# Cross-attention queries split batch by batch, first tile's by GpSimd, contexts loaded ahead of weights, norms of the last tile in pieces

## What is computed

```python
x = x + _L0_xattn_ref(_layernorm(x, axis=-1), ctx_768, Wq, Wk, Wv, Wo, bo)
x = x + _L0_attn_ref(_layernorm(x, axis=-1), Wq, Wk, Wv, Wo, rel_bias_emb)
x = x + _L0_ffn_ref(_layernorm(x, axis=-1), clip_x, clip_down, w_gate, w_up, w_down)
...
# in _L0_xattn_ref, per head:
scores = jnp.einsum("bhsd,bhkd->bhsk", q, k) * scale
probs = jax.nn.softmax(scores, axis=-1)
out = jnp.einsum("bhsk,bhkd->bhsd", probs, v)
...
# in _L0_ffn_ref:
xq = _act_fake_quant(x, clip_x[0])
gate = jnp.einsum("bsh,ih->bsi", xq, _weight_fake_quant(w_gate))
up = jnp.einsum("bsh,ih->bsi", xq, _weight_fake_quant(w_up))
h = _act_fake_quant(jax.nn.silu(gate) * up, clip_down[0])
return jnp.einsum("bsi,hi->bsh", h, _weight_fake_quant(w_down))
```

## Time and profile before

| | |
|---|---|
| median of 3 runs | 1633.85 us (1632.8 to 1635.03) |
| the profiled execution | 1636.37 us, span 1634.5 us |
| mean granted clock of TensorE | 0.987 |
| busy share of the span | TensorE 96%, its weight loads 79%, VectorE 68%, ScalarE 45%, GpSimd 22% |
| chain that ended last | TensorE 68%, VectorE 12%, issue 12%, ScalarE 4%, DMA 3% |

### The profile page before, as it was taken

How to read it: one execution, slowest core, us unless ns; L and a number is a source line. 1 busy time by engine, 2 the same in 40 slices (tenths; PEclk the granted TensorE clock), 3 DMA queues, 4 the chain that set the end, 5 groups by cost and what they waited for, 6 DMA issues and landing times.

```text
span 1634.5 us, 33087 instructions
## 1 busy us (share of the span) xinstructions
PE 1566.0 (96%) x12242; PEld 1299.2 (79%) x12242; DVE 1114.9 (68%) x2348; ACT 734.6 (45%) x1555; POOL 355.8 (22%) x217
## 2 busy tenths in 40 slices
PE   7999869999999999999999998899999999997989
PEld 6888758888988889888998887777878778775444
DVE  7776656676667766677666776657657665566788
ACT  5554554555545554455545553333122222222755
POOL 0000234443444335343443433000000000000000
PEclk9999999999999999999999999999999999998999
DMA  6898853332333223342333312250310311324022
GB/s 245 321 357 340 322 192 121 134 114 73 137 132 134 85 91 133 133 148 62 114 133 133 137 57 103 78 194 21 103 67 27 118 39 39 115 90 171 1 103 104
DMA packets 80030, 213.37 MB, mean 131 GB/s; under 512 B 5776, under 2 KB 31824, under 8 KB 77136
## 3 DMA queue, kind: packets, MB, share of 16 engines
q1 hardware_dynamic: 79952, 212.27, 36.0%
HBM read 141.86 MB, written 70.39 MB: 130 GB/s over the span
## 4 chain that ended last, share of the span: by engine, by line
PE 68%; DVE 12%; issue 12%; ACT 4%; DMA 3%; SPq 0%; DVEq 0%; POOL 0%; ACTq 0%; POOLq 0%
PE psum_o L663 13%; PE psum_s L640 6%; PE psum_q L640 6%; PE psum_o L678 5%; PE psum_o L1331 5%; PE psum_q L1331 5%; PE psum_o L532 5%; PE psum_q L1371 4%; PE psum_t L1399 4%; PE psum_t L651 2%; DVE qk L1001 2%; PE psum_t L611 2%; PE psum_s L1385 2%; ACT qk L782 1%; PE psum_t L564 1%
## 5 line engine op out<-in xcount | busy, mean ns | idle before, releaser
L663 PE MATMUL psum_o<-pT,c_nat 128*128 128x512 f32 x1152 | 314.1, 410 | 15.4 <-issue 12.2
L663 PEld LDWEIGHTS psum_o<-pT,c_nat 128*128 128x128 f32 x1152 | 207.6, 193 | 51.8 <-DVE pT L900 14.8
L1183 POOL TENSOR_TENSOR c_nat<-c_raw,zero 128x768 fp32r<-128x768 f32 x64 | 95.4, 1490 | 638.0 <-PE psum_o L663 465.4
L1067 DVE TENSOR_SCALAR oT<-psum_o,c_last 128x512 f32<-128x512 f32 x192 | 143.4, 747 | 72.7 <-PE psum_o L663 72.7
L640 PE MATMUL psum_s<-cT,qk 128*128 128x258 f32 x1152 | 170.3, 290 | 5.8 <-DVE qk L1001 1.9
L640 PEld LDWEIGHTS psum_s<-cT,qk 128*128 128x128 f32 x1152 | 153.0, 191 | 15.5 <-DVE cT L900 6.1
L841 ACT ACTIVATE probs<-psum_s,nmax 128x257 f32<-128x257 f32 x128 | 61.1, 478 | 210.9 <-DVE nmax L1082 210.9
L640 PE MATMUL psum_q<-cT,qk 128*128 128x258 f32 x1152 | 154.9, 286 | 0.0
L640 PEld LDWEIGHTS psum_q<-cT,qk 128*128 128x128 f32 x1152 | 144.0, 190 | 5.1 <-issue 5.1
L900 DVE TENSOR_TENSOR pT<-psum_t,pT 128x512 fp32r<-128x512 f32 x128 | 87.7, 686 | 73.5 <-ACT pT L740 73.5
L740 ACT ACTIVATE cT<-psum_t 128x256 fp32r<-128x256 f32 x192 | 67.6, 389 | 126.6 <-PE psum_t L611 126.4
(11 more groups left out here) (263 smaller groups left out, 3101.7 us busy)
## 6 DMA issues: line engine op xcount, KB each, us to landing
qk_by_tile<-staged SPq DMA_DIRECT2D x32, 1536.0 KB, 9.9
raw<-qk_by_tile SPq DMA_DIRECT2D x16, 3072.0 KB, 12.7
c_raw<-in_ctx_dram SPq DMA_DIRECT2D x64, 384.0 KB, 3.3
last_row<-in_ctx_dram SPq DMA_DIRECT2D x64, 192.0 KB, 4.2
out_dram<-x_out SPq DMA_DIRECT2D x32, 256.0 KB, 2.0
x_res<-in_x_dram SPq DMA_DIRECT2D x16, 256.0 KB, 2.6
x_in<-out_dram SPq DMA_DIRECT2D x4, 1024.0 KB, 8.0
x_res<-out_dram SPq DMA_DIRECT2D x16, 256.0 KB, 2.8
```

The lines of the kernel that those rows point to most:

```text
L663: i = pe.matmul(ps[:], c_nat[(b - 1) % 2][:, part, k, m * P:(m + 1) * P], pT[:, moving, k, :], start=(k, part, moving) == (0, 0, 0), stop= ...
L1067: nc.vector.tensor_scalar(oT[:, m, :, (b - 1) % 4, :], ps[:].rearrange("p (s q) -> p s q", q=SQ), c_last[:, (b - 1) % 2, m:m + 1], None, A ...
```

## The change

- Queries are split per batch and score group, in 16 instructions of 128x384 per tile and part instead of four of 128x1536. In batches 1 to 3 of a tile the parts for the next tile's batches 0 to 2 are made (in batch 3 ScalarE also makes those of batch 3, whose low parts follow in the next tile's batch 0). TensorE waits for each score group's part.
- In the first tile GpSimd makes both parts of batches 0 to 2, and the low part of the output weights. Group 3 of the projection has all its `Q` chunks first and then all its `QK` chunks.
- GpSimd subtracts the next context's last key before it splits the present one, not after.
- SyncE loads contexts and tile 1's queries ahead of the weights.
- In the last tile the statistics and the norm are spread in pieces over batches 1 to 3, and w2q's low part comes at the tile's end.
- The reloads for the feed-forward part are spread over three output tiles, and 54 transposes whose result nobody reads stand in three places of TensorE's queue.

```diff
+        if s == 3:
+            u += [(("Q", s, j), ("o0", "o1")[j % 2]) for j in range(4, 8)]
+            u += [(("CT", "start", c), ("t0", "t1")[c % 2]) for c in range(3)]
         for gp in range(2):
-            if gp:
+            if gp and s < 3:
                 u += [(("Q", s, j), ("o0", "o1")[j % 2]) for j in range(4, 8)]
...
-            if b == 0:
-                pe.wait_ge(s_qlo, 4 * t + (rg + 1))
+            pe.wait_ge(s_qlo, 16 * t + 4 * b + (rg + 1))
             ps, done = empty(pe, U1(("S", b, rg), t, section))
...
+        def raw_of(b, rg):
+            return raw[:, :, rg, :].rearrange("p h (c b q) -> p b c h q", c=KC, q=SQ)[:, b, :, :, :]
+        def qk_of(part, b, rg):
+            return qk[:, part, rg, :, b, :].rearrange("p c (h q) -> p c h q", h=4)
+        def act_qk_high(act, t, b):
             act.wait_ge(s_qraw, 16 * t + 16)
-            nc.scalar.activation(qk[:, 0, rg, :, :, :].rearrange("p c b (h q) -> p h (c b) q", h=4),
-                                 raw[:, :, rg, :].rearrange("p h (a q) -> p h a q", q=SQ), ACT.Copy).then_inc(s_qhi, 1)
+            for rg in range(4):
+                nc.scalar.activation(qk_of(0, b, rg), raw_of(b, rg), ACT.Copy).then_inc(s_qhi, 1)
...
+            act.wait_ge(s_qhi, 12)
+            act_qk_high(act, 0, 3)
...
                 if after:
                     ctxT(b, 2)
-                if section == "first" and b in (1, 2):
-                    act_wo_high(act, b - 1)
+                if b and more:
+                    act_qk_high(act, t + 1, b - 1)
+                if b == 3 and more:
+                    act_qk_high(act, t + 1, 3)
+                if section == "first" and b >= 2:
+                    act_wo_high(act, b - 2)
...
+        def dve_qk_low(dve, t, b, groups):
+            for rg in groups:
+                dve.wait_ge(s_qhi, 16 * t + 4 * b + (rg + 1))
+                nc.vector.tensor_tensor(qk_of(1, b, rg), raw_of(b, rg), qk_of(0, b, rg).bitcast(F32),
+                                        ALU.subtract).then_inc(s_qlo, 1)
...
-                qk_next = b == 3 and more
+                qk_next = b > 0 and more
                 row_max(b, 0)
+                if b == 0:
+                    dve_qk_low(dve, t, 3, range(2))
                 if section == "first" and b == 0:
                     nc.vector.memset(cT[1][:, :, :, 2 * P:SKP].bitcast(F32), 0.0).then_inc(s_zero, 1)
                 if before:
                 row_max(b, 1)
                 if before:
                     dve_probsT(dve, t, b, 1, section)
+                if b == 0:
+                    dve_qk_low(dve, t, 3, range(2, 4))
                 inverse(b, 0)
                 if b == 1 and begun:
                     dve_wv(dve, t, 0, section)
                 inverse(b, 1)
                 if b == 1 and begun:
                     dve_wv(dve, t, 1, section)
+                if not more and b == 2:
+                    dve_group_stats(dve, GROUPS, x_in2, range(2, GROUP))
+                if not more and b == 3:
+                    rsqrt_turn(own_ln, group_ln, group)
                 row_max(b, 3)
                 inverse(b, 2)
-                if qk_next:
-                    dve_qk_low(dve, t + 1, 0, section)
                 if before:
                     dve_attended(dve, t, b, 0, section)
                 inverse(b, 3)
-                if qk_next:
-                    dve_qk_low(dve, t + 1, 1, section)
+                if not more and b == 3:
+                    dve_group_norm(dve, GROUPS, x_in2, x_in2, range(2))
                 if after:
                     ctxT(b, 0)
                     ctxT(b, 1)
                 norm(b, 2)
                 norm(b, 3)
+                if not more and b == 2:
+                    rsqrt_start(own_ln, group_stats, group_ln, group)
                 if before:
                     dve_attended(dve, t, b, 1, section)
                 if qk_next:
-                    dve_qk_low(dve, t + 1, 2, section)
-                    dve_qk_low(dve, t + 1, 3, section)
+                    dve_qk_low(dve, t + 1, b - 1, range(2))
                 if not more and b == 3:
-                    dve_weight(dve, "q")
+                    dve_group_norm(dve, GROUPS, x_in2, x_in2, range(2, GROUP))
                 if b == 3 and begun:
                     dve_x_out(dve, t, section)
                 if after:
                     ctxT(b, 2)
                 if before:
                     dve_attended(dve, t, b, 2, section)
-                if section == "first" and b >= 2:
-                    dve_wo_low(dve, b - 2)
+                if qk_next:
+                    dve_qk_low(dve, t + 1, b - 1, range(2, 4))
                 if not more and b == 1:
-                    dve_group_stats(dve, GROUPS, x_in2)
-                    dve_group_rsqrt(dve, GROUPS)
+                    dve_group_stats(dve, GROUPS, x_in2, range(2))
                 if not more and b == 2:
-                    dve_group_norm(dve, GROUPS, x_in2, x_in2)
+                    for _ in range(2):
+                        rsqrt_turn(own_ln, group_ln, group)
+            if not more:
+                dve_weight(dve, "q")
...
+        def pool_first_queries(pool, b):
+            G = nc.gpsimd
+            nothing = zero[:].rearrange("p (a b c) -> p a b c", a=1, b=1).to_broadcast([P, KC, 4, SQ])
+            for rg in range(4):
+                G.tensor_tensor(qk_of(0, b, rg), raw_of(b, rg), nothing, ALU.add).then_inc(s_qhi, 1)
+            for rg in range(4):
+                pool.wait_ge(s_qhi, 4 * b + (rg + 1))
+                G.tensor_tensor(qk_of(1, b, rg), raw_of(b, rg), qk_of(0, b, rg).bitcast(F32), ALU.subtract).then_inc(s_qlo, 1)
+        def pool_wo_low(pool, h):
+            pool.wait_ge(s_wohi, h + 1)
+            part = slice(4 * h, 4 * h + 4)
+            nc.gpsimd.tensor_tensor(wo_low[:, part, :], wo_raw[:, part, :], wo_high[:, part, :].bitcast(F32),
+                                    ALU.subtract).then_inc(s_wolo, 1)
+        def pool_first_tile(pool):
+            pool_less_last(pool, 0, 0)
+            pool_less_last(pool, 0, 1)
+            full(pool, project(("Q", GROUPS - 1, 7)))
+            pool.wait_ge(s_qraw, 16)
+            for b in range(3):
+                pool_first_queries(pool, b)
+            pool_split(pool, 0, 0, "first")
+            full(pool, U1(("S", 0, 0), 0, "first"))
+            pool_split(pool, 0, 1, "first")
+            for b in range(2, 4):
+                pool_less_last(pool, 0, b)
+                pool_split(pool, 0, b, "first")
+            pool_less_last(pool, 0, 4)
+            for h in range(2):
+                pool_wo_low(pool, h)
         def pool_cross_tile(pool, t, section):
-            if section == "first":
-                pool_less_last(pool, t, 0)
             for b in range(4):
-                pool_split(pool, t, b, section)
                 if section != "last" or b < 3:
                     pool_less_last(pool, t, b + 1)
-                if b == 1 and section != "first":
+                pool_split(pool, t, b, section)
+                if b == 1:
                     pool_bias(pool, t)
...
+        def sp_first_tile(sp):
             sp.wait_ge(s_nat, 1)
             load_ctx(sp, 0, 2)
+            sp.wait_ge(s_qlo, 16)
+            load_qk(sp, 0, 1)
+            sp.wait_ge(s_nat, 2)
+            full(sp, U1(("CT", 0, 2), 0, "first"))
+            load_ctx(sp, 0, 3)
             for i in range(4):
                 sp.wait_ge(s_staged[i], 32 * GROUPS)
-            sp.dma_start(wv[:], Wv.rearrange("(k p) n -> p k n", p=P)).then_inc(s_wvo, 16)
-            sp.dma_start(wo_raw[:], Wo.rearrange("(k p) n -> p k n", p=P)).then_inc(s_wvo, 16)
-            sp.dma_start(bo_all[:], bo.rearrange("(a n) -> a n", a=1).to_broadcast([P, D])).then_inc(s_wvo, 16)
+            sp.dma_start(wo_raw[:], Wo.rearrange("(k p) n -> p k n", p=P)).then_inc(s_wo, 16)
+            sp.dma_start(bo_all[:], bo.rearrange("(a n) -> a n", a=1).to_broadcast([P, D])).then_inc(s_wo, 16)
             sp.dma_start(x_res[:], rows(x_rows, 0)).then_inc(s_xres, 16)
+            sp.wait_ge(s_nat, 3)
+            load_ctx(sp, 0, 4)
+            sp.dma_start(wv[:], Wv.rearrange("(k p) n -> p k n", p=P)).then_inc(s_wv, 16)
+            sp.wait_ge(s_nat, 4)
+            load_ctx(sp, 0, 5)
...
-                        sp.dma_start(wdT[:].rearrange("p c k n -> p c (k n)"), wd_dram.rearrange("c p n -> p c n")).then_inc(s_wguback, 16)
                         sp.dma_start(wguT[:].rearrange("p c w k n -> p c (w k n)"), wgu_dram.rearrange("c p n -> p c n")).then_inc(s_wguback, 16)
+                    if not more and i == 1:
                         sp.wait_ge(s_x3st, 16 * (GROUPS - 1))
                         sp.dma_start(xn3_all[:, 0:GROUP * (GROUPS - 1), :].rearrange("p (s t) d -> p s (t d)", t=GROUP),
                                      xn3_dram.rearrange("s p n -> p s n")).then_inc(s_x3back, 16)
+                    if not more and i == 2:
```

(13 more changed lines are left out.)

149 lines of the change are left out of this document (68 added, 81 removed).

## The result

| | before | after | ratio |
|---|---|---|---|
| median | 1634.44 us (1632.8 to 1637.21) | 1780.05 us (1767.27 to 1784.57) | 1.0875 (1.0835 to 1.0915) |
| profiled span | 1634.5 us | 1782.8 us | |
| mean granted clock | 0.987 | 0.981 | |

A forecast was written before the change was run, and what follows sets the result against it. TensorE was taken to bound the loop, with 0.73 us of reserve for the row maximum. 1636.4 - 6 + 122 + 17 - 4 - 3 = 1762, 1760 against the median; own range 1715 to 1810, given range down to 1640.

The forecast's parts named there:

- row maximum, batch 2 to 3: Loop, end of a batch: VectorE's row maximum starts 4.9 us after the batch's scores start (S), instead of 1.28.
- value product, inner steps: Loop, batch 1 to 2 and 2 to 3: TensorE's value product comes 3.0 us later each, S+8.2 against S+5.18.
- value product, boundary: Loop, batch 3 to the next tile: value product at S+8.25 against S+5.55, 2.7 us later.
- batch 0: Loop, first batch of a tile: adds no low split at its end and catches up, so no loss.
- one tile: Cross-attention loop: each tile grows by 8.7 us from 51.79, 122 us over 14 tiles.
- half clock in the loop: Loop: TensorE's idle gaps bring half clock, 1.6 us each; a quarter of the gaps taken, 17 us, between 0 and 67.
- to batch 1 of tile 1: Start through the first tile: batch 1 of tile 1 reached at about 254.5 instead of 260.4, gain 6 (16 to -4).
- last tile: Last tile: some 13.5 us above regular batches before, loss 9.5 after, so gain 4 us (0 to 9).
- behind the last tile: Feed-forward: transposes fill the first gap, gain 2 us (-2 to 3); with the down product and spread reloads, 3 together.
- Rival 2: Loop: nothing is held for pieces this small, only the order costs; +11 us, so 1645; chance 0.07.
- leaving an end out of the range: Loop, batch boundaries: a further 1.85 us GpSimd instruction in the way, 5.6 us more a tile, 200 in all; excluded.
- the played-out line: Loop, batch's end: GpSimd's add delayed to 639.5, its subtract between third and fourth low splits, row maximum at 643.7.

The follow-up runs named there:

- the short context split: Changed kernel, order untouched, but from the second tile on GpSimd splits only 4 of each 384 context columns: 1661.92 us, ratio 1.0164.
- the subtraction moved alone: Kernel before, with only GpSimd's last-row subtraction put ahead of its context split from the second tile on: 1656.98 us, ratio 1.0125.
- both orders undone: Changed kernel with queries again split in four 128x1536 pieces and GpSimd's context split again ahead of its subtraction, from the second tile on: 1627.14 us, ratio 0.9950.
- The kernel that splits by rows: Changed kernel with the next tile's queries again split in four 128x1536 pieces in the last batch, from the second tile on: 1646.52 us, ratio 1.0072.
- the last experiment: Kernel with batch-wise queries and GpSimd's order undone and w2q's low part back ahead of the output sum, now without unread transposes: 1622.68 us, ratio 0.9917.

## Why the prediction was right, step by step

| step | forecast, us | measured, us |
|---|---|---|
| row maximum, batch 2 to 3 | S+4.9 | S+4.45 |
| value product, inner steps | +3.0 each | +2.5 each |
| value product, boundary | +2.7 | +2.45 |
| batch 0 | 0 | +2.0 |
| one tile | +8.7 | +9.69 |
| 14 tiles | +122 | +135.7 |
| half clock in the loop | +17 | +15.9, 13 tiles, this execution |
| to batch 1 of tile 1 | -6 | +0.1 |
| last tile | -4 | -2.1 |
| behind the last tile | -3 | -1.6 |

The mechanism was right: GpSimd and VectorE held each other an instruction at a time, and the subtraction came in between the third and fourth piece. The holding, the moved subtraction and the two orders have an experiment each (the short context split, the subtraction moved alone, both orders undone); that the subtraction comes in between those two pieces is read from the trace. Rival 2's rest of 2.4 us a tile without holding was measured as 2.6, but its working does not give 2.4: its row maximum at S+2.6 (measured S+2.5) costs 0.7 us a step, 2.1 in three.

That 1760 came so near the 1780 is in part luck. Batch 0's 28 us were missing from the sum, and the three steps at the batches' ends were put some 14 us too high in all. The quarter of the gaps for the half clock was a guess; in the profiled execution it was 10 stretches behind 39 gaps.

Three steps failed. **"Batch 0 adds no low split at its end and catches up":** it has low splits in its middle, and the same change moves GpSimd's subtraction onto them; 2.0 us a tile, 28 in all. I had used that move only as an argument for leaving an end out of the range. Its price with no other part of the change, where it meets the large splits of batch 3 and not these, is 1.5 us a tile and 21 us in all.

**The first tile's 6 us:** up to tile 1's first row maximum 5.4 us were won, but its first batch took 15.03 us instead of 9.53. The cause is the wo_low piece, which the prediction listed without following what it holds:

```profile
248.60 4.58 POOL L1228 TENSOR_TENSOR wo_low<-wo_raw,wo_high 128x2048 fp32r<-128x2048 f32 x1 [6.21 <-ACT wo_high L838]
...
251.03 4.64 DVE L1018 TENSOR_TENSOR qk<-raw,qk 128x384 fp32r<-128x384 f32 x2
...
255.31 0.66 PE L616 MATMUL psum_t<-ident,c_raw 128*128 128x128 f32 x4 [2.40 <-POOL c_raw L1192]
```

VectorE's two pieces took 4.64 us behind it, and GpSimd's next subtraction was late for TensorE. TensorE's waits there are 1.24 and 2.40 us, with half clock behind them. The kernel that splits by rows has no pieces at that place, and the same batch took it 10.69 us. The 4.9 us for one wo_low piece was about right (4.58); that it would hold VectorE for that long was not drawn.

**The last tile:** the wait behind w2q's low part was forecast 3.9 us longer and came out 5.1 longer (6.68 against 1.62 in the kernel before), since the splits themselves took 5.55 us, not the 4.48 of the earlier trace rows. That is the same holding once more: GpSimd's addition of the bias, 1.28 us from 1185.55, stands in between the two splits, and the second is recorded at 3.35 us instead of 2.28. The 13.5 us that the prediction starts from are some 1.7 more than the terms it names (6.15 and 2.71 of waits, some 1.3 and 1.6 of half clock). The feed-forward gain was mis-sized by 1.4. From the first quantized transposes on it is 2.3 us, and by the last experiment it comes from the unread transposes; 0.7 us were lost ahead of them, for which no run shows a cause.

Where the inner steps are 0.5 us short of the forecast, the delay of the add is one part: VectorE's second piece held it for 0.2 us (1.66 against 1.47), not for the 0.4 of the played-out line.

Left open: why the clock falls in some tiles and not in others with the same instructions and nearly the same waits.

## What to carry to other kernels

Before splitting an engine's work into pieces and spreading them, list what the other engine runs at each new place: VectorE and GpSimd excluded each other for whole instructions here, and most of the cost (7.1 of 9.7 us a tile) came from what stood in between two pieces, not from the pieces. The same sixteen pieces cost 9.7 us a tile in one order of the two queues and gained 0.35 in another. A move on an engine that is 20% busy is not free if that engine can hold a busy one. And an experiment that makes one instruction shorter also moves the others: read where the second collision went before the whole gain is put down to the first.

## What the runs showed of the hardware

- VectorE instructions with only SBUF tensors waited for a running GpSimd instruction and the other way round, with two tensors read (0.55 us alone, up to 2.20) and with one (0.40 us, up to 2.02; the scalings, 1.80 us for two instead of 0.61). Those with a PSUM operand ran beside it at their usual length (0.42 and 0.74 us at 611.31 and 611.64).
- Who asks first runs first: GpSimd's subtraction asked 0.1 us ahead of VectorE at 598.10, and VectorE was stopped once; in the changed kernel it asked 0.5 us behind VectorE's third piece (612.80 against 612.30), and VectorE was stopped twice.
- Cutting each of two GpSimd instructions into four made them alternate with VectorE's; it did not shorten the sum of TensorE's waits (3.60 and 3.79 us against 4.38 and 2.03).
- A half-clock stretch of 3.41 us cost 1.6 us of time in the loop, and in the changed kernel such stretches came behind waits of 1.6 to 2 us; other waits of that length had none behind them.
